# Second-matrix products of the feed-forward layers wait row by row, and a phase's last tiles are made two at a time

## What is computed

```
xn = layernorm(x)
x  = x + attn0(xn) + ffn0(xn)     # ffn0: square(relu(xn W1^T)), RMS norm, ternary weights, hidden width 1024
xn = layernorm(x)
x  = x + attn1(xn) + ffn1(xn)     # ffn1: (sigmoid(xn W1^T) * xn W2^T) W3^T, ternary weights, hidden width 704
```

## Time and profile before

| | us |
|---|---|
| median of 3 runs | 1327.66 (1326.15 to 1327.93) |
| profiled execution | 1328.96 |
| its span | 1327.2 |
| PE busy | 1200.7 (90% of the span) |
| DVE busy | 896.5 (68%) |
| ACT busy | 751.5 (57%) |
| POOL busy | 547.1 (41%) |

### The profile page before, as it was taken

One profiled execution on the slowest core, in us unless ns is written; L12 is line 12 of the kernel. 1 busy time (PEld: TensorE's weight loads), 2 busy tenths in 40 slices (PEclk: granted clock), 3 DMA queues, 4 the chain that ended last, 5 costly groups with the idle time before them and its releaser, 6 DMA issues.

```text
span 1327.2 us, 22453 instructions
## 1 busy us (share of the span) xinstructions
PE 1200.7 (90%) x7552; PEld 856.9 (65%) x7552; DVE 896.5 (68%) x2308; ACT 751.5 (57%) x1700; POOL 547.1 (41%) x567
## 2 busy tenths in 40 slices
PE   4888779999999889887799999999999999999898
PEld 3776744444443477776567776777777777777688
DVE  6867587899997344444577666677766667777743
ACT  2466216677776424545466656666665566666632
POOL 2435233444441100607065554556655445565310
PEclk9898756899998797888899999999999999999999
DMA  6773154454540284021211111110111121011315
GB/s 187 147 147 59 45 73 58 59 80 81 76 64 3 68 236 137 31 85 48 76 29 44 45 45 43 30 33 29 44 45 45 49 87 33 29 45 33 128 38 185
DMA packets 112466, 93.55 MB, mean 70 GB/s; under 512 B 49696, under 2 KB 102240, under 8 KB 110560
## 3 DMA queue, kind: packets, MB, share of 16 engines
q1 hardware_dynamic: 112352, 92.11, 29.6%
HBM read 53.02 MB, written 30.67 MB: 63 GB/s over the span
## 4 chain that ended last, share of the span: by engine, by line
PE 35%; DVE 11%; issue 3%; ACT 1%; DMA 0%; ACTq 0%; DVEq 0%
PE psum L1025 11%; PE psum L1073 9%; PE psum L194 8%; PE psum L1046 7%; DVE a_part L938 3%; DVE psum L943 3%; DVE a_pt L976 2%; DVE w L2289 1%; ACT a_p L990 1%; DVE w_lat L2289 1%; DVE q00l L2289 1%; DVE q01l L2289 1%; DVE a_nm L943 1%; DMA w<-wf_d 0%; DVE ql1l L2170 0%
## 5 line engine op out<-in xcount | busy, mean ns | idle before, releaser
L1007 POOL TENSOR_SCALAR a_p<-a_p,a_rl 128x128 f32<-128x128 f32 (+7 forms) x256 | 218.8, 856 | 307.5 <-DVE a_rl L949 307.5
L990 ACT ACTIVATE a_p<-psum,a_nm 128x128 f32<-128x128 f32 (+7 forms) x256 | 189.7, 741 | 55.7 <-DVE a_nm L943 54.1
L1508 ACT ACTIVATE a_pt<-psum 128x512 f32<-128x512 f32 (+3 forms) x384 | 167.9, 492 | 80.0 <-PE psum L1371 77.5
L1046 PE MATMUL psum<-ident,a_p 128*128 128x128 f32 x1152 | 175.4, 279 | 14.2 <-DVE a_pt L976 14.2
L976 DVE COPY a_pt<-psum 128x512 f32<-128x512 f32 (+1 forms) x192 | 114.5, 596 | 109.0 <-PE psum L1046 108.5
L974 ACT ACTIVATE a_pt<-psum 128x256 f32<-128x256 f32 (+2 forms) x192 | 87.5, 456 | 164.0 <-PE psum L1046 163.9
L1046 PEld LDWEIGHTS psum<-ident,a_p 128*128 128x128 f32 x1152 | 127.2, 140 | 62.3 <-issue 47.7
L1073 PE MATMUL psum<-a_pt,v 128*64 128x256 f32 (+1 forms) x1280 | 159.4, 370 | 1.4 <-ACT rows_k L1087 1.4
L1361 PE MATMUL psum<-a_op_k,a_op_q 64*128 64x512 f32 (+3 forms) x384 | 137.4, 456 | 9.1 <-ACT a_op_q L1527 8.1
L1371 PE MATMUL psum<-a_op_q,a_op_k 64*128 64x512 f32 (+3 forms) x384 | 132.6, 432 | 7.5 <-ACT a_pt L1508 6.2
L1371 PEld LDWEIGHTS psum<-a_op_q,a_op_k 64*128 64x128 f32 x384 | 65.1, 201 | 104.4 <-ACT a_pt L1508 88.4
(11 more groups left out here) (389 smaller groups left out, 2907.7 us busy)
## 6 DMA issues: line engine op xcount, KB each, us to landing
ot_d<-rows_k SPq DMA_DIRECT2D x16, 512.0 KB, 4.5
a_swap<-w_p SPq DMA_DIRECT2D x60, 128.0 KB, 2.3
rows_q<-qk_d SPq DMA_DIRECT2D x48, 128.0 KB, 4.5
rows_k<-qk_d SPq DMA_DIRECT2D x48, 128.0 KB, 7.5
w<-wf_d SPq DMA_DIRECT2D x15, 384.0 KB, 3.4
qk_d<-d_stage_h SPq DMA_DIRECT2D x64, 64.0 KB, 2.1
qk_d<-d_stage_l SPq DMA_DIRECT2D x64, 64.0 KB, 2.1
d_x<-in_L_attn_x_dram SPq DMA_DIRECT2D x8, 256.0 KB, 7.2
```

Source lines behind the costliest of these rows:

```text
L990: e.activation(s.p[:, t % NPB, 0:(i + 1) * P], C.score[t % 2][:, 0:(i + 1) * P], ACT.Exp, scale=-1.0, bias=s.nm[:, k:k + 1], accum_out=s.l ...
L1007: e.tensor_scalar(s.p[:, t % NPB, 0:(i + 1) * P], s.p[:, t % NPB, 0:(i + 1) * P], s.rl[:, k:k + 1], 1.0, ALU.mult, ALU.mult).then_inc(s.no ...
L1046: ins = e.transpose(C.turn[par][:, (k - k0) * P:(k - k0 + 1) * P], s.p[:, tt % NPB, k * P:(k + 1) * P], C.ident[:, :])
L1508: e.activation(pt[:, k // G0 % NPT, hd, off:HALF], bank_b("score", g, k)[:, off:HALF], ACT.Exp, scale=-1.0).then_inc(exped, 1)
```

## The change

Three things are changed, all in the products with the second matrix; the number and the shapes of the products stay.

- `dense0`, `drop(b, c, 0)`: the first tile of a half waits for the first 6 blocks, makes their 12 products, waits for block 7, makes 2, waits for block 8, makes 2. The other three tiles are as before.
- `dense0`, end of batch 1 (`drop_last`): tiles 0 and 2, which lie in different banks, are made side by side in three such pieces; then the square sums, then tiles 1 and 3. DVE's wait for tiles 4 and 5 of batch 1 is one higher, since tile 5 is now the third to be done.
- `feed1`, `drop(c)` for both halves: tiles 0 and 2 side by side, after 4 blocks, 5 blocks and 6 blocks, then tiles 1 and 3. DVE's waits for `down` follow the new order: 3 for the first bank of a half, 4 for the second.

```diff
+                def made(b, c, m):
+                    e.wait_ge(high, b * N_F + c * NH0 + m)
+                    e.wait_ge(low, b * N_F + c * NH0 + m)
+
+                def partial(b, c, i, first, end):
+                    q = slice(i * P, (i + 1) * P)
+                    for m in range(first, end):
+                        room = (b * N_F + c * NH0 + m) % ROOMS_H
+                        e.matmul(down_place(4 * c + i), h_h[:, room, q], w2[:, m, :], start=m == 0, stop=False)
+                        ins = e.matmul(down_place(4 * c + i), h_l[:, room, q], w2[:, m, :], start=False, stop=m == NH0 - 1)
+                    return ins
+
                 def drop(b, c, i):
                     if i == 0:
-                        e.wait_ge(high, b * N_F + (c + 1) * NH0)
-                        e.wait_ge(low, b * N_F + (c + 1) * NH0)
                         if b:
                             e.wait_ge(added, 4 * (c + 1))
-                    q = slice(i * P, (i + 1) * P)
-                    accumulate(e, down_place(4 * c + i),
-                               [(part[:, (b * N_F + c * NH0 + m) % ROOMS_H, q], w2[:, m, :])
-                                for m in range(NH0) for part in (h_h, h_l)]).then_inc(down, 1)
+                        made(b, c, NH0 - 2)
+                        partial(b, c, i, 0, NH0 - 2)
+                        made(b, c, NH0 - 1)
+                        partial(b, c, i, NH0 - 2, NH0 - 1)
+                        made(b, c, NH0)
+                        partial(b, c, i, NH0 - 1, NH0).then_inc(down, 1)
+                    else:
+                        partial(b, c, i, 0, NH0).then_inc(down, 1)
+
+                def drop_last(b, c):
+                    e.wait_ge(added, 4 * (c + 1))
+                    for k0, k1 in ((0, NH0 - 2), (NH0 - 2, NH0 - 1), (NH0 - 1, NH0)):
+                        made(b, c, k1)
+                        for i in (0, 2):
+                            ins = partial(b, c, i, k0, k1)
+                            if k1 == NH0:
+                                ins.then_inc(down, 1)
...
-                drop(1, 1, 0)
+                drop_last(1, 1)
                 square_sums(1, 1)
-                for i in range(1, 4):
+                for i in (1, 3):
                     drop(1, 1, i)
...
-                        e.wait_ge(down, b * NT + 2 * (tt // 2) + 2)
+                        out_of_turn = b == B - 1 and tt // 2 == 2
+                        e.wait_ge(down, b * NT + 2 * (tt // 2) + 2 + out_of_turn)
...
-            e.wait_ge(high, (c + 1) * HT1)
-            e.wait_ge(low, (c + 1) * HT1)
-            for i in range(4):
-                tt = 4 * c + i
-                q = slice(i * P, (i + 1) * P)
-                accumulate(e, down_bank[tt][:, (tt % 2) * E:(tt % 2 + 1) * E],
-                           [(hh[m][:, q], W.w3[:, m, :]) for m in range(HT1) for hh in (h_h, h_l)]).then_inc(down, 1)
+            for k0, k1 in ((0, HT1 - 2), (HT1 - 2, HT1 - 1), (HT1 - 1, HT1)):
+                e.wait_ge(high, c * HT1 + k1)
+                e.wait_ge(low, c * HT1 + k1)
+                for i in (0, 2):
+                    partial(e, c, i, k0, k1)
+            for i in (1, 3):
+                partial(e, c, i, 0, HT1)
...
-            e.wait_ge(down, tt + 1 if tt % 2 else tt + 2)
+            e.wait_ge(down, 4 * (tt // 4) + 3 + tt % 4 // 2)
```

More of the change, by code:

```diff
@@ L1937, in drop, with partial @@
                     e.wait_ge(sem, value)
-            e.wait_ge(high, (c + 1) * HT1)
-            e.wait_ge(low, (c + 1) * HT1)
-            for i in range(4):
-                tt = 4 * c + i
-                q = slice(i * P, (i + 1) * P)
-                accumulate(e, down_bank[tt][:, (tt % 2) * E:(tt % 2 + 1) * E],
-                           [(hh[m][:, q], W.w3[:, m, :]) for m in range(HT1) for hh in (h_h, h_l)]).then_inc(down, 1)
+            for k0, k1 in ((0, HT1 - 2), (HT1 - 2, HT1 - 1), (HT1 - 1, HT1)):
[5 more added lines that the diff above has]
+                partial(e, c, i, 0, HT1)
+        def partial(e, c, i, first, end):
+            tt = 4 * c + i
+            q = slice(i * P, (i + 1) * P)
+            place = down_bank[tt][:, (tt % 2) * E:(tt % 2 + 1) * E]
+            for m in range(first, end):
+                e.matmul(place, h_h[m][:, q], W.w3[:, m, :], start=m == 0, stop=False)
+                ins = e.matmul(place, h_l[m][:, q], W.w3[:, m, :], start=False, stop=m == HT1 - 1)
+            if end == HT1:
+                ins.then_inc(down, 1)
         for n in range(len(jobs)):
```

## The result

The changed kernel takes 1304.74 us in the median of 4 runs (1299.95 to 1312.07), the kernel before 1326.91 in the 4 runs beside them (1323.18 to 1327.93). The ratio is 0.9856 with a 95% interval of 0.9815 to 0.9896: 14 to 25 us less. A second series of 6 runs gave 1304.30 and a ratio of 0.9843 (0.9805 to 0.9880), 16 to 26 us less.

A forecast was written before the change was run, and what follows sets the result against it. PE's products at each phase's end, waiting for the last rest rows, were taken as the bound. Gains (a) to (f) less 0.2 cost sum to 17.6 us; from 1328.96, then 1.3 for the median, this gives 1310.1, forecast 1310, range 1305 to 1318.

The forecast's parts named there:

- (a): Layer 0, first half of batch 0: twelve products go before the last row; gain 0.2 us, not more than 0.3.
- (b): Layer 0, second half of batch 0: 14 products start at once, square sums then wait for `joined`; gain 3.2 us (2.0 to 4.8).
- (c): Layer 0, first half of batch 1: 12 products go after `added`, before the late rows; gain 2.8 us (1.5 to 3.1).
- (d): End of layer 0: two tiles start on six blocks, the tail starts earlier; gain 4.6 us (2.4 to 6.3).
- (e): Layer 1, batch 0, middle and end: products start on four blocks during the idle time; gain 4.0 us (2.6 to 4.1).
- (f): Layer 1, batch 1: 0.5 us in the middle, 2.5 at the end; gain 3.0 us (2.6 to 3.1).
- the 3 to 4 named as a sign: Layer 1, both batches: the transposes should come 3 to 4 us sooner after the last lift.
- Costs: Split tiles' added waits: 0 to 1 us, 0.2 in the sum; alternating two banks: zero.
- Clock as before: Rival, chance 0.15: slow stretches keep their length, only idle time is won, 10.3 us, giving 1317.
- Given back: Rival, chance 0.04: gains of (b) and (c) end in another wait, only the phases' ends count, near 1320.
- slower rival: Chance 0.03: split work and changing banks keep the clock at half for all products with the second matrix, 1343.
- No effect: Rival, chance 0.03: the first six rows come as late as the last; the same time, 1327.

The follow-up runs named there:

- sums later: Changed kernel with only the square sums of batch 0's second half made one lift later: 1305.93 us (4 runs), ratio 0.9857.
- rows in layer 0 alone: Kernel before with row-by-row waits in layer 0 only, single tiles in the old order, layer 1 as before: 1315.89 us (10 runs), ratio 0.9933.
- order only: Changed kernel's tile order and bank alternation, but every half waits for all its rows first, as before: 1318.04 us (10 runs), ratio 0.9964.

## Why the prediction was right, and where it was off

**(a) First wait, 0.2.** Not to be separated: the first square sums come 1.9 us sooner, 1.5 of them from ahead of the change.

**(b) Second wait, forecast 3.2 (2.0 to 4.8).** Against the profile that the sum was made on: from the end of lift 19 to the start of lift 23 it took 18.3 us before and 15.0 after, 3.3 less. Each step of it is there: 14 products at once, two idle times of 0.8 and 0.9 us, the square sums held by `joined`, one low stretch of 3.4 us. But the base was one execution of an uncertain thing. The old waits took 18.3, 18.4, 15.5 and 14.0 us in their four profiles, mean 16.5, as the clock was at half for long, for long, shortly, and not at all. The new order took 15.0 in five out of five. Against the mean the gain is 1.5, so that 3.3 met the 3.2 of the sum was luck. The new order takes away less time than uncertainty: with its square sums straight after the idle time it never kept its clock here, which "sums later" did.

**(c) Third wait, forecast 2.8 (1.5 to 3.1).** 7.5 us before (7.5 to 7.9 in four profiles) from the last lift's end to the next lift's start, 4.7 after. The clock did not fall. Right; against the mean of the four (7.7) it is 3.0.

**(d) End of layer 0, forecast 4.6 (2.4 to 6.3).** From the last lift's end to the first attention 21.7 us in three profiles of the old code, 16.9 to 17.0 in six with the new waits and 18.7 in the seventh (rows in layer 0 alone): 4.8, and 3.0 in the seventh. The one short low stretch that I assumed is the one at 144.4. The reason given for two tiles side by side did not count in the one single-tile profile with the same short low stretch: one tile does the same there.

**(e), (f) Layer 1, forecast 4.0 and 3.0.** 3.8 and 2.8 in the first pair of profiles, 3.8 and 2.9 in the means (60.8 and 68.1 against 56.7 to 57.5 and 65.0 to 65.3). Part of (e) was luck too. The sum took 1.4 us for the low stretch at the end of batch 0, which only the first profile has: from the end of the lift to the transposes it took 10.0 us there, 8.7 in the three other profiles of the old code in layer 1, and 6.3 with the change. These three waited longer in the middle of the batch instead (0.6 to 1.0 us for the last row, and not 0.29), so that the batch's gain came out the same. In batch 1 the transposes come 2.4 us sooner behind the last lift (9.7 and 7.3), not the 3 to 4 named as a sign.

**Costs.** Four more waits at each split tile and the change of banks: nothing seen at a change of bank, the step is 0.12 us in pairs; the first step after a real wait takes 0.19 us at full clock, inside time that was idle before.

**The sum.** 17.6 was forecast. By the means of the stretches, 9.6 in layer 0 (1.5 + 3.0 + 0.3 between + 4.8), 3.8 and 2.9 make 16.3. The runs say more: 1304.4 us in the mean of ten runs, 1323.6 and 1324.8 in the runs of before beside the experiments, 19 to 20 us. The intervals of the two ratios reach from 14 to 26 us, and 16.3 lies in both, near their lower ends. The step that was short is the one that put the forecast at 1310: the sum was made against one execution of 1328.96, and I took the difference from the median of three runs for all there is of chance. Beside the experiments the kernel before ran from 1315.56 to 1332.81, with a granted clock from 0.936 to 0.953, in 36 runs with a mean of 1324.0. So of the 5.7 us between 1310.1 and 1304.4, 3.7 are the base and 2.0 the gain. The 0.2% that a measurement was said to tell was too good as well: the intervals here are some 0.4% to either side.

The mean clocks of the runs divide the gain. Through the 36 runs of before goes a line by which a thousandth less in mean clock is 0.9 us more. At the same clock the ten runs of the changed kernel are 11.7 us shorter. Their mean clock is 0.953 and not 0.944, which makes the other 8 us. The forecast had 10.3 for idle time alone (its low ends) and 7.3 for the clock, so both parts came about as reckoned. The clock's part can be seen in the changed place: over layer 0's stretch the mean granted clock was 0.82 to 0.86 in the four profiles with the old waits and 0.91 to 0.97 in the seven with the new. Whether the 3 us above the sum of the stretches are chance or a gain of the changed timing in the first attention stays open.

**The rivals.** "Clock as before" is out where it could be seen: the low stretches became shorter in (c) and (d) each time, and by the runs some 8 us of the gain are the clock's. "Given back" is out: the second attention's 673.5 to 674.2 us do not depend on when it starts, and behind (b) and (c) all came sooner. The slower rival fell with "order only". The rule named beside it (the Trainium skill, page "TensorE: Matmul & The Clock Gate", section "A second HAM failure mode: psum-queue depth-cycling"), of a kernel that cycled through PSUM banks with short idle times between its groups, is shown by no run here: where the bank changes after every two products they stay 0.12 us apart, and "order only" had no lower clock than the kernel before. "No effect" fell with the first product at 104.28, straight behind the lift.

## What to carry to other kernels

A product sum that waits for all its inputs at once can start on those that are there: move the wait down to the last rows, count what is made meanwhile, and read which wait stands next (here DVE's sum in front of the square sums). Making a second tile beside the first is worth something only where one tile's products do not fill the time to the last row, so reckon them at the clock that is granted there. And take a second profile of the unchanged kernel before crediting or pricing a stretch where the clock changes.

## What the runs showed of the hardware

The granted clock differs between executions of the same code after the same idle time: after 2.49 us of it PE's clock was at half for 10.2 us (in two profiles), for 3.4 us or not at all. It also falls where PE hardly idles: in the first attention of the kernel before it was 0.51 over 20 us, with PE busy 19.7 of them and 27.6 of the 29 us ahead, while the changed kernel, busy 27.3 of the same 29, kept its full clock through the 20 us behind them. Most products there contract over 64 rows or write 32 columns. The kernel before spread by 1.3% from run to run, and with it went its mean clock.

In layer 0, DVE operations on 128x512 values took 0.68 us away from POOL's squaring and from 0.68 to 1.52 us beside it, and 0.68 beside POOL's memsets. So a POOL job that looks like a delay (the memsets) can be what keeps two engines apart.
